# Slots' first weights in two-row and one-row loads over 64 partitions, and four PSUM banks for one attention's values

## The chip, the cores and the metric

One core of a Trainium2 chip runs the whole program in one launch. The metric is the device time of that launch in microseconds. TensorE (PE) has two queues in the profile: PE for matmuls and PEld for weight loads. DVE is VectorE, ACT is ScalarE, POOL is GpSimd, and SP and ACT issue nearly all DMAs. All arithmetic is in float32.

## The reference

The program is a small early-fusion transformer on 16 sequences of 102 tokens (25 image patches and 77 words) with 192 features. Four layers follow the embedding, each an attention-like block and a feed-forward block, with a residual and a layer norm before each. Two blocks matter here.

The first feed-forward block is a soft mixture of 64 slots. Each token is normalised and compared with 64 slot vectors; a softmax over tokens gives the dispatch weights, a softmax over slots the combine weights.

```python
y = einsum('bts,btd->bsd', dispatch_w, x)            # 64 slots of 192 features for each sequence
y = einsum('sif,bsi->bsf', fc1_weight, y) + fc1_bias # own 192 x 768 weights for each slot
y = gelu(y)
y = einsum('sfo,bsf->bso', fc2_weight, y) + fc2_bias # own 768 x 192 weights for each slot
out = einsum('bsd,bst->btd', y, combine_w)
```

Each slot's weights are used for 16 rows only, so the block reads 2 x 64 x 192 x 768 numbers, 75.5 MB, once.

The third attention (layer 2) has 12 heads of 64 features, without biases:

```python
q, k, v = heads(x @ w_q), heads(x @ w_k), heads(x @ w_v)   # 192 -> 12 x 64
out = merge(softmax(q @ k.T / 8) @ v) @ w_o + b_o
```

## The kernel before

Tokens of one sequence lie on 102 partitions. Four sequences make a group, and there are four groups; most stages are loops over groups. Each engine has its own written-out program; semaphores join them. PSUM has eight banks, named by use: `SBANKS` (0, 1) for scores, `TBANKS` (2, 3) for transposes, `OBANKS` (4, 5) for outputs, `XBANKS` (6, 7), and `FBANKS`, which are 2, 3, 6 and 7. `claim(banks)` on TensorE takes the next bank of the tuple and waits until its last contents have been read; `filled` says that it is full; on DVE and ACT `full` waits for that, and `free` gives the bank back.

**Slots.** After the first attention each group's tokens are normalised on DVE (`turn_d`, L1068 multiplies by the norm's weight and writes the features in the order p, k, where feature k x 96 + p becomes column 2p + k). TensorE then makes the dispatch products: for each sequence L2211 with columns 0 to 127 of the tokens as its 128 wide weights and 64 slots as moving columns, and L2215 with columns 128 to 191. ACT copies the result to `YTF` (128 rows, every slot) and `YTH` (even slots on partitions 0 to 63, odd slots on 64 to 127).

The slots are then worked through in 16 quads of four. For each quad, `into_slots` multiplies by first weights (L2232 with the 128 rows, L2236 with the 64 others, L2238 adds the bias), ACT applies Gelu, `turn_hidden` transposes, and one quad later `out_of_slots` (L2248) multiplies by second weights. Three buffers (`QRING`) hold the weights of three quads. The first three quads' weights are loaded beforehand, quads 1 and 2 from the end of the first attention on. From quad 3 on SP loads first weights (`load_first`) as soon as TensorE has given the buffer back (`fc1_used`), and ACT, after Gelu of a quad, loads second weights for the one two ahead (`load_second`).

In DRAM a slot's first weights are rows p of 0 to 96, each with both k, so 2 x 768 numbers: 6 KB that lie together. Row 96 is the bias. `load_first` takes the rows (p, k) as 192 rows of 3 KB. The first 128 of the four slots go to 128 partitions in one DMA of 1536 KB (`FULL`), the last 64 in two DMAs of 384 KB (`HALF`), for the even slots to partitions 0 to 63 and for the odd to 64 to 127. Second weights are one DMA of 2304 KB over 128 partitions, with rows of 4.5 KB for each slot, in two of the three buffers, and four of 576 KB in the third.

**Third attention's values.** In its loop over groups, TensorE makes queries and keys into `FBANKS`, then for each of the four sequences ("batch" `bb`) the values: it claims both `OBANKS`, fills each with 6 heads (384 columns, L1941 for 128 features, L1945 for the other 64), and goes to the next sequence. DVE's `values(V, 64, None)` copies the banks to `V` in the same order (L1006). Then both enter `attention`. Its scores alternate between the banks 0 and 1, and before the first of each TensorE waits until the bank's last contents are read. The product with the values comes five steps later and waits for the last two value banks (`v_moved[-2:]`).

## Time and profile before

| what | value |
|---|---|
| median of 3 runs | 1671.95 us (1662.51 to 1679.76) |
| profiled execution | 1669.09 us |
| its span, first to last instruction | 1667.1 us |
| mean granted TensorE clock | 0.908 of 2.4 GHz |
| busy, share of the span | PE 84%, PEld 59%, DVE 41%, ACT 40%, POOL 23% |
| DMA over the span | 178.84 MB, 107 GB/s |
| slots' stage, first matmul into a slot to the last quad | about 340 to 555 us |
| third attention | about 1070 to 1330 us |

The span is what the profiler sees between the first and the last instruction; 2.0 us of the execution's time lie outside it. A granted clock of 1.00 is 2.4 GHz and 0.50 is 1.2 GHz.

### The profile page before, as it was taken

How to read it: one execution, taken by the hardware profiler on the slowest of the kernel's cores; microseconds unless marked ns; L12 is line 12 of the kernel's file. 1: busy time of each engine (PE TensorE's matmuls, PEld its weight loads, DVE VectorE, ACT ScalarE, POOL GpSimd, SP SyncE). 2: the span in 40 equal slices, each digit the busy share in tenths (PEclk: the TensorE clock that was granted, in tenths of full speed). 3: DMA queues.
4: the chain of work that ended last, by engine and by line, in shares of the span. 5: the costliest groups of instructions: out<-in, count | busy, mean ns of one | idle time of the engine just before them, and what ended most of it. 6: DMA issues, size and time to landing. Idle time of an engine off the chain costs nothing.

```text
span 1667.1 us, 31759 instructions
## 1 busy us (share of the span) xinstructions
PE 1404.5 (84%) x10300; PEld 984.7 (59%) x10300; DVE 683.6 (41%) x2124; ACT 673.0 (40%) x2261; POOL 385.9 (23%) x467
## 2 busy tenths in 40 slices
PE   6799997798566877888899899688988999889994
PEld 4566665633122434555578799454654666679993
DVE  5557756611101277444433622333542423551113
ACT  1667664410000143888842022153654643213331
POOL 5213222200000132232200266220220200124441
PEclk8999996577778778999998899799999999989997
DMA  8434331759999400000004366200000020136653
GB/s 221 138 85 125 91 97 48 232 180 365 301 311 307 140 24 1 1 0 0 0 0 128 105 200 194 75 1 1 0 0 0 16 117 0 31 107 189 187 169 105
DMA packets 96071, 178.84 MB, mean 107 GB/s; under 512 B 36570, under 2 KB 56312, under 8 KB 94336
## 3 DMA queue, kind: packets, MB, share of 16 engines
q1 hardware_dynamic: 81776, 130.75, 27.0%
q10 hardware_dynamic: 7056, 30.67, 5.6%
q0 software_dynamic: 7136, 16.10, 3.1%
q8 instruction: 57, 0.93, 0.3%
q14 instruction: 46, 0.38, 0.1%
HBM read 150.50 MB, written 26.99 MB: 106 GB/s over the span
## 4 chain that ended last, share of the span: by engine, by line
PE 55%; DVE 13%; issue 12%; DMA 9%; ACT 7%; SPq 2%; POOL 1%; DVEq 0%; ACTq 0%; POOLq 0%
DMA WM<-in_fc 8%; PE bank L2444 6%; PE bank L1941 6%; PE bank L2430 4%; PE bank L2014 4%; PE bank L2026 4%; PE bank L2043 3%; PE bank L1945 3%; PE bank L2434 3%; PE bank L2053 3%; PE bank L2104 2%; PE bank L1989 2%; PE bank L2096 2%; ACT ON L1674 2%; ACT KZ L1815 2%
## 5 line engine op out<-in xcount | busy, mean ns | idle before, releaser
L1941 PE MATMUL bank<-XT,AREA 128*128 128x408 f32 (+1 forms) x320 | 138.3, 557 | 23.0 <-ACT XT L1618 10.1
L2014 PE MATMUL bank<-KZ,QT 128*102 128x102 f32 x1152 | 140.2, 261 | 12.2 <-ACT PB L1674 7.4
L700 POOL TENSOR_TENSOR PB<-PB,RCU 102x306 f32<-102x306 f32 x96 | 69.3, 722 | 310.1 <-DVE RCU L964 310.0
L2014 PEld LDWEIGHTS bank<-KZ,QT 128*102 128x102 f32 x1152 | 121.0, 173 | 31.5 <-issue 15.5
L684 POOL TENSOR_TENSOR RS<-VE,expo 102x4 f32<-102x4 f32 (+1 forms) x53 | 53.1, 1002 | 361.7 <-DVE VE L904 303.6
L2444 PE MATMUL bank<-WM,KZ 128*128 x660 | 118.2, 327 | 0.0
L1941 PEld LDWEIGHTS bank<-XT,AREA 128*128 128x128 f32 (+1 forms) x320 | 56.2, 196 | 89.6 <-issue 69.4
L2444 PEld LDWEIGHTS bank<-WM,KZ 128*128 128x128 f32 x660 | 105.7, 190 | 0.4
L1655 ACT ACTIVATE KZ<-bank,AREA 128x128 f32<-128x128 f32 x198 | 54.8, 375 | 121.4 <-PE bank L2434 121.4
L2043 PE MATMUL bank<-PT,V 102*32 102x102 f32 (+1 forms) x1152 | 85.9, 270 | 15.2 <-DVE OT L974 12.3
L2026 PE MATMUL bank<-AREA,OT 128*102 128x192 f32 x384 | 88.9, 345 | 11.3 <-DVE SLOTS L1329 5.3
L1668 ACT ACTIVATE PT<-bank 102x306 f32<-102x306 f32 x192 | 86.3, 452 | 26.2 <-PE bank L2053 25.7
L1784 ACT ACTIVATE QT<-bank 128x512 f32<-128x512 f32 (+1 forms) x32 | 15.7, 491 | 195.9 <-PE bank L2238 195.9
L821 POOL DMA_INDIRECT rows_out<-KZ,TARGET x66 | 66.7, 1010 | 118.3 <-DVE KZ L1474 74.1
L1674 ACT ACTIVATE PB<-bank,MXU 102x102 f32<-102x102 f32 x192 | 65.9, 377 | 64.6 <-DVE MXU L958 64.6
L700 POOL TENSOR_TENSOR ON<-ON,RCU 102x306 f32<-102x306 f32 x96 | 67.1, 699 | 92.5 <-DVE RCU L964 92.2
L2430 PE MATMUL bank<-KZ,SLOTS 128*128 128x128 f32 x660 | 84.6, 275 | 2.6 <-issue 2.6
L2430 PEld LDWEIGHTS bank<-KZ,SLOTS 128*128 128x128 f32 x660 | 82.0, 192 | 3.4 <-issue 3.4
L809 POOL DMA_INDIRECT KZ<-rows_in,TOKEN x66 | 67.7, 1026 | 53.0 <-DVE TOKEN L1451 33.5
L1945 PE MATMUL bank<-XT,AREA 64*128 64x408 f32 (+1 forms) x320 | 78.6, 569 | 0.0
L1267 DVE COPY QT<-bank 128x192 f32<-128x192 f32 x16 | 5.7, 357 | 177.5 <-PE bank L2248 177.5
L958 DVE TENSOR_REDUCE MXU<-bank 102x3 f32<-102x306 f32 x128 | 60.9, 476 | 41.2 <-PE bank L2014 37.4
(347 smaller groups left out, 2807.3 us busy)
## 6 DMA issues: line engine op xcount, KB each, us to landing
AREA<-in_fc SPq DMA_DIRECT2D x10, 1536.0 KB, 20.3
SLOTS<-in_m3w SPq DMA_DIRECT2D x33, 384.0 KB
WM<-in_fc ACTq DMA_DIRECT2D x5, 2304.0 KB, 18.9
WM<-in_fc SPq DMA_DIRECT2D x6, 1536.0 KB, 24.1
AREA<-in_fc ACTq DMA_DIRECT2D x4, 2304.0 KB, 20.5
SLOTS<-in_m1w SPq DMA_DIRECT2D x33, 256.0 KB
AREA<-pos_scratch SPq DMA_DIRECT2D x16, 459.0 KB
pos_scratch<-AREA SPq DMA_DIRECT2D x8, 913.5 KB
```

The source lines that it names most:

```text
L700: pool.tensor_tensor(p, p, scale, ALU.mult).then_inc(sem["probs_ready"], 1)
L809: pool.indirect_dma_start(XG[i % XRING], None, rows_in, bass.IndirectOffsetOnAxis(ap=TOKEN[:, i:i + 1], axis=0), bounds_check=NB * T - 1, ...
L821: pool.indirect_dma_start(rows_out, bass.IndirectOffsetOnAxis(ap=TARGET[:, i:i + 1], axis=0), YO[i % YRING], None, bounds_check=2 * NB * T ...
L1668: free(activation(PT[s % 2][:, 0:HPU, :], src, ACT.Copy), k)
L1674: last = activation(p, p if pos else psum[k][0:T, cols(j)], ACT.Exp, scale=-1.0, bias=MXU[:, s % 4, j:j + 1], accum_out=SMU[:, s % 4, j:j ...
L1941: last = pe.matmul(dst, *whole(n), start=n < 2, stop=False)
L1945: return [pe.matmul(dst, *part(n), start=False, stop=n >= len(outs) - 2) for n, dst in enumerate(outs)]
L2014: last = pe.matmul(psum[k][0:T, cols(j)], QT[:, tile, cols(bb)], KALL[:, unit % per_tile * (HEADS // per_tile) + tile, cols(bb)], start=Tr ...
L2026: last = pe.matmul(psum[PROJBANK][0:T, 0:D], OT[bb % 2][:, m, :], wo[:, m, :], start=m == 0, stop=m == parts - 1)
L2043: last = pe.matmul(psum[k][row:row + rows, cols(tile)], by_head(dv)[:, bb * HEADS + h, :], PT[n % 2][:, j, :], start=True, stop=True)
L2430: pe.matmul(p[:, c], w_all[:, (j * per + m) * 128:(j * per + m + 1) * 128], x[:, 0:TILE], start=m == 0, stop=False)
L2444: last = pe.matmul(p[:, 0:D], HG[i % HRING][:, f * 128:(f + 1) * 128], w2[:, bass.ds(e, 1), f * D:(f + 1) * D].rearrange("p o d -> p (o d) ...
```

## The change

First weights: each slot is loaded by two DMAs. Rows p of 0 to 63, both k together, go as 6 KB rows to 64 partitions (384 KB); rows 64 to 95 go as 64 rows of 3 KB to the other 64 partitions (192 KB). For even slots the two-row part is on partitions 0 to 63, for odd slots on 64 to 127. A quad takes eight DMAs, and `fc1_loaded` counts to 128 for a quad in place of 48. A pair of slots shares one piece of 3 x 768 columns in each buffer: the even slot has columns 0 to 2 x 768, the odd slot from 768 on, or from 2 x 768 on where it has one row. The sizes and the places of the three buffers stay as they are.

`into_slots` has the same matmuls. One takes 128 partitions (one k of the two-row half, and all single rows on the other half), the other takes 64 (the other k of the two-row half). The features of tokens and of slot vectors are put in the matching order: k = 0 of p below 64, then the (p, k) rows of p from 64 on, then k = 1 of p below 64. That takes two DVE operations where one was. In the dispatch products the odd slots need other columns of the tokens than the even, so each sequence has two products with 32 columns where it had one with 64.

Values: the third attention's values use the four banks 4, 5, 0, 1 in turn, on TensorE and on DVE. The product with the values waits for the last four fillings.

```diff
+VBANKS = OBANKS + SBANKS
...
         def load_first(engine, q):
-            j, s = q % QRING, RING * q
-            rows = t["fc1"][s:s + RING].rearrange("s p k f -> (p k) s f")
-            engine.dma_start(FULL[j], rows[0:128]).then_inc(sem[f"fc1_loaded{j}"], 16)
-            for odd in range(2):
-                engine.dma_start(HALF[j][64 * odd:64 * odd + 64], rows[128:D, odd:RING:2]
-                                 ).then_inc(sem[f"fc1_loaded{j}"], 16)
+            j = q % QRING
+            for r in range(RING):
+                slot, odd, there = t["fc1"][RING * q + r], r % 2, FIRST[j][r // 2]
+                engine.dma_start(there[64 * odd:64 * odd + 64, FF * odd:FF * odd + 2 * FF],
+                                 slot[0:64].rearrange("p k f -> p (k f)")).then_inc(sem[f"fc1_loaded{j}"], 16)
+                engine.dma_start(there[64 - 64 * odd:128 - 64 * odd, 2 * FF * odd:2 * FF * odd + FF],
+                                 slot[64:KD].rearrange("p k f -> (p k) f")).then_inc(sem[f"fc1_loaded{j}"], 16)
...
                 for first in range(0, GB * HEADS, per):
-                    k = at.bank(OBANKS)
+                    k = at.bank(OBANKS if dv == 16 else VBANKS)
...
-                weight = nw0[:].rearrange("t (k p) -> t k p", k=2).unsqueeze(1).to_broadcast([T, GB, 2, KD])
-                give(tt(XND[g][:].rearrange("t b (p k) -> t b k p", k=2), X1[:].rearrange("t b (k p) -> t b k p", k=2),
-                        weight, ALU.mult), "xn_ready")
+                weight = nw0[:].rearrange("t (k p) -> t k p", k=2).unsqueeze(1)
+                src = X1[:].rearrange("t b (k p) -> t b k p", k=2)
+                tt(XND[g].rearrange("t b (n c) -> t b n c", c=64)[:, :, 0:3:2, :], src[:, :, :, 0:64],
+                   weight[:, :, :, 0:64].to_broadcast([T, GB, 2, 64]), ALU.mult)
+                give(tt(XND[g][:, :, 64:128].rearrange("t b (p k) -> t b k p", k=2), src[:, :, :, 64:KD],
+                        weight[:, :, :, 64:KD].to_broadcast([T, GB, 2, KD - 64]), ALU.mult), "xn_ready")
...
                 for bb in range(GB):
-                    c = bb * NSLOT
-                    pe.matmul(p[:, c:c + NSLOT], x[:, bb, 0:128], DW[g % 2][:, bb, :], start=True, stop=True)
+                    for odd in range(2):
+                        pe.matmul(p[:, bb * NSLOT + odd:(bb + 1) * NSLOT:2], x[:, bb, 64 * odd:64 * odd + 128],
+                                  DW[g % 2][:, bb, odd:NSLOT:2], start=True, stop=True)
...
-                pe.wait_ge(sem[f"fc1_loaded{j}"], 48 * (q // QRING + 1))
+                pe.wait_ge(sem[f"fc1_loaded{j}"], 128 * (q // QRING + 1))
...
-                    two_banks = [claim(OBANKS) for _ in range(2)]
+                    two_banks = [claim(VBANKS) for _ in range(2)]
...
-                attention(2, 64, wo2, v_moved[-2:])
+                attention(2, 64, wo2, v_moved[-4:])
```

## Rows read from the trace of the kernel before

**Rows 1.** The page's chain that ended last, by line.
```profile
DMA WM<-in_fc 8%; PE bank L2444 6%; PE bank L1941 6%; PE bank L2430 4%; PE bank L2014 4%; PE bank L2026 4%; PE bank L2043 3%; PE bank L1945 3%; PE bank L2434 3%; PE bank L2053 3%; PE bank L2104 2%; PE bank L1989 2%; PE bank L2096 2%; ACT ON L1674 2%; ACT KZ L1815 2%
```

**Rows 2.** The page's DMA issues: count, KB each, us to landing.
```profile
AREA<-in_fc SPq DMA_DIRECT2D x10, 1536.0 KB, 20.3
...
AREA<-in_fc ACTq DMA_DIRECT2D x4, 2304.0 KB, 20.5
...
AREA<-in_fc SPq DMA_DIRECT2D x10, 384.0 KB, 25.0
```

**Rows 3.** Timeline of the issuing queues: start us, us, instruction.
```profile
294.79 0.58 SPq L226 DMA_DIRECT2D AREA<-in_fc  x1
295.40 1.37 SPq L228 DMA_DIRECT2D AREA<-in_fc  x2
...
360.39 0.44 ACTq L239 DMA_DIRECT2D WM<-in_fc  x1
```

**Rows 4.** Windows, slots' stage: busy times, then TensorE clock, DMA share, GB/s.
```profile
297.00:300.50 3.50, 1.26 (x9) 0.90 (x8) 3.08 (x9) 1.36 (x8) 0.20 (x1) 0.50 1.00 394
301.00:304.00 3.00, 2.36 (x15) 2.18 (x13) 1.29 (x10) 1.88 (x10) 2.19 (x3) 0.50 1.06 234
306.50:310.50 4.00, 3.89 (x30) 3.71 (x31) 2.24 (x6) 0.93 (x6) 0.34 (x1) 0.50 1.00 408
381.50:388.50 7.00, 3.66 (x58) 2.45 (x58) 1.82 (x5) 0.38 (x1) 0.00 (x0) 1.00 1.04 297
389.50:396.50 7.00, 6.04 (x22) 1.09 (x26) 0.00 (x0) 0.21 (x1) 0.00 (x0) 0.52 1.02 417
432.00:437.00 5.00, 1.52 (x22) 0.96 (x12) 1.82 (x5) 0.00 (x0) 0.00 (x0) 1.00 1.06 199
350.50:545.50 195.00, 138.09 (x1286) 52.76 (x1285) 24.86 (x68) 13.74 (x28) 0.00 (x0) 0.80 1.01 315
460.00:540.00 80.00, 51.78 (x464) 19.52 (x460) 9.11 (x25) 4.91 (x10) 0.00 (x0) 0.78 1.03 311
```

**Rows 5.** Waits of PE, 350 to 553 us, and its timeline in quads 2 and 3.
```profile
PE bank L2232 <- DMA KZ<-in_fc: 25.4, 4, 8.2
PE bank L2232 <- DMA AREA<-in_fc: 21.1, 3, 7.8
PE bank L2232 <- DMA WM<-in_fc: 11.7, 4, 6.9
...
361.36 1.06 PE L2232 MATMUL bank<-AREA,SLOTS 128*32 128x512 f32 x8
...
369.27 1.07 PE L2232 MATMUL bank<-WM,SLOTS 128*32 128x512 f32 x8
```

**Rows 6.** DMA queues, 365 to 370 us: packets, MB, share of busy time.
```profile
q1 hardware_dynamic: 190, 0.53, 38.8%
```

**Rows 7.** Timeline of one group's dispatch.
```profile
306.61 1.78 PEld L2211 LDWEIGHTS bank<-PT,XN 102*128 102x128 f32 x8 [0.68 <-ACT PT L1773]
306.61 1.97 PE L2211 MATMUL bank<-PT,XN 102*128 102x64 f32 x8 [0.47 <-ACT PT L1773]
...
308.23 0.96 DVE L1068 TENSOR_TENSOR ON<-X,early 102x768 f32<-102x768 f32 x1
```

**Rows 8.** Timeline of third attention's values, first group.
```profile
1091.14 1.25 DVE L1006 COPY V<-bank 102x384 f32<-102x384 f32 x2 [10.81 <-PE bank L1945]
...
1092.45 1.54 PE L1941 MATMUL bank<-AREA,XT 128*102 128x384 f32 x4 [1.34 <-DVE V L1006]
...
1093.91 0.89 PE L1945 MATMUL bank<-AREA,XT 64*102 64x384 f32 x4
...
1102.59 1.15 DVE L1006 COPY V<-bank 102x384 f32<-102x384 f32 x2 [2.51 <-PE bank L1945]
1103.87 1.07 DVE L958 TENSOR_REDUCE MXU<-bank 102x3 f32<-102x306 f32 x2
```

**Rows 9.** Waits over the whole span.
```profile
PE bank L1941 <- DVE V L1006: 16.3, 12, 1.7
```

More of the change, by code:

```diff
@@ L210, in build @@
         HS = HT.rearrange("p k t -> p (k t)")[:, 0:FT * 128].rearrange("p (k t) -> p k t", k=FT)
-        FULL = [buf[:, 0:RING * FF].rearrange("p (s f) -> p s f", s=RING) for buf in (WM, AREA)]
-        HALF = [buf[:, RING * FF:6 * FF].rearrange("p (s f) -> p s f", s=2) for buf in (WM, AREA)]
+        PAIR = 3 * FF
         SECOND = [[buf[:, 6 * FF + r * FT * D:6 * FF + (r + 1) * FT * D] for r in range(RING)] for buf in (WM, AREA)]
@@ L216, in build, with first_rows @@
         flat_of_all = lambda buf, c, n: buf.rearrange("p k t -> p (k t)")[:, c:c + n]
[L217 to L219 removed]
+        FIRST = [[buf[:, 0:PAIR], buf[:, PAIR:2 * PAIR]] for buf in (WM, AREA)]
+        FIRST.append([AREA[:, taken:taken + PAIR], flat_of_all(KT, 0, PAIR)])
+        SECOND.append([WM[:, taken:taken + FT * D], AREA[:, taken + PAIR:taken + PAIR + FT * D],
                        flat_of_all(HT, FF, FT * D), flat_of_all(QT[:], FF + D, FT * D)])
+        def first_rows(j, r, c0, c1):
+            at0 = 2 * FF * (r % 2)
+            rows = slice(64 * (r % 2), 64 * (r % 2) + 64)
+            return FIRST[j][r // 2][:, at0 + c0:at0 + c1], FIRST[j][r // 2][rows, FF + c0:FF + c1]
         def load_first(engine, q):
[L224 to L229 removed]
+            j = q % QRING
[5 more added lines that the diff above has]
+                                 slot[64:KD].rearrange("p k f -> (p k) f")).then_inc(sem[f"fc1_loaded{j}"], 16)
         def load_second(engine, q):
@@ L1035, in unit_slots @@
                 step(dve.reciprocal(RC[0:NSLOT, 0:1], MX[0:NSLOT, 0:1]))
-                give(ts(SL2.rearrange("s (p k) -> s k p", k=2), SL.rearrange("s (k p) -> s k p", k=2),
+                src = SL.rearrange("s (k p) -> s k p", k=2)
+                ts(SL2.rearrange("s (n c) -> s n c", c=64)[:, 0:3:2, :], src[:, :, 0:64],
+                   RC[0:NSLOT, 0:1], slS[:, 0:1], ALU.mult, ALU.mult)
+                give(ts(SL2[:, 64:128].rearrange("s (p k) -> s k p", k=2), src[:, :, 64:KD],
                         RC[0:NSLOT, 0:1], slS[:, 0:1], ALU.mult, ALU.mult), "xn_ready")
@@ L2214, in _ @@
                     for odd in range(2):
-                        last = pe.matmul(p[64 * odd:64 * odd + 64, c:c + NSLOT // 2], x[:, bb, 128:D],
+                        last = pe.matmul(p[64 * odd:64 * odd + 64, c:c + NSLOT // 2], x[:, bb, 128 - 128 * odd:D - 128 * odd],
                                          DW[g % 2][:, bb, odd:NSLOT:2], start=True, stop=True)
@@ L2232, in into_slots @@
                         pe.matmul(o[32 * r:32 * r + 32], YTF[:, NB * s:NB * s + 32],
-                                  FULL[j][:, r, c0:c1], start=True, stop=False)
+                                  first_rows(j, r, c0, c1)[0], start=True, stop=False)
                     for r in range(RING):
@@ L2236, in into_slots @@
                         pe.matmul(o[32 * r:32 * r + 32], YTH[rows, NB * (s // 2):NB * (s // 2) + 32],
-                                  HALF[j][rows, r // 2, c0:c1], start=False, stop=False)
+                                  first_rows(j, r, c0, c1)[1], start=False, stop=False)
                     filled(pe.matmul(o, PICK[:, 128 * q:128 * q + 128], BIAS[:, c0:c1], start=False, stop=True), k)
```

3 lines of the change are left out of this document (removed).

## The prediction

> **What bounds the kernel now.** I read the page's chain first, then windows of the stage that it names, then the timeline of the other places that the diff touches. TensorE is the busiest engine over the span, but the chain by line [rows 1] has as its largest single item the load of the slots' weights, 8% of the span, before any matmul line. The windows [rows 4] show that stage: from 350.5 us, when the first buffer is given back, to 545.5 us the DMA engines are busy without a gap (share 1.01) and move 315 GB/s, 61.4 MB in 195 us, which is the 13 quads after the first three at 2304 KB of first and 2304 KB of second weights each [rows 2]. TensorE needs 7.9 us for a quad at full clock (quads 2 and 3 begin at 361.4 and 369.3 us) and waits 58 us in all for first weights [rows 5]. At the lower clock level (0.50 to 0.52 [rows 4]) it needs at most 16 us, still less than the 17 that I get below for a quad's loads. So a change in the rate of these loads passes straight into the time, and a change in TensorE's work inside the stage doesn't.
>
> The rate isn't one number, and this carries the prediction. SP puts a 128-partition load of 1536 KB and then two 64-partition loads of 384 KB on its queue for each quad [rows 2, 3]. When the queue works alone, 297 to 300.5 us is the wide load: 394 GB/s. Right behind it, 301 to 304 us, are the two narrow ones: 234 GB/s at the same full share [rows 4]; from 352 us on, at the next refill, the pair repeats. The rows in DRAM are 3 KB in both; what differs is the partitions written. Once ACT's queue runs beside it (its loads are all of 128 partitions) the same alternation goes on: 297 GB/s in a stretch of narrow loads, 417 in the next (three of the slow and two of the fast kind by 405 us); later the stretches blur into a steady 311 [rows 4].
>
> **The change, slots' loads.** Eight loads for a quad in place of three, all of them over 64 partitions: four of 384 KB in 6 KB rows, four of 192 KB in 3 KB rows. The 1536 KB at 128 partitions are gone. Two effects are to be priced.
> Longer rows: second weights have 4.5 KB rows, and on SP's queue alone they moved at 408 GB/s [rows 4], against 394 for 3 KB rows. Half as long again bought 3%, within what the edges of such windows are worth, so 6 KB rows get nothing from me; by the same 3% on half the bytes it would be 3 us.
> Narrow loads: while a load writes one half of the partitions, that half takes all of SP's bytes and half of ACT's. In a slow stretch, 365 to 370 us, SP's queue had 39% of the DMA engines' time and so nearly of the bytes [rows 6], ACT's the rest, so the loaded half took 0.39 + 0.305 = 0.69 of 297 GB/s, 205 GB/s. In the new kernel both queues have 2304 KB a quad, so the share is 0.5 + 0.25 = 0.75, and the total 205 / 0.75 = 274 GB/s. SP's queue is alone for the first 10 us (ACT issues first at 360.4 us [rows 3]) and moves 2.3 MB there at 234 GB/s; the other 59.1 MB at 274 take 216 us. Together 226 against 195: **+31 us**, 17 us for a quad. The ends: with 234 GB/s as what a half can take, 312 in total, 199 us, +4; with 199 GB/s, the slowest stretch of narrow loads [rows 4], 265 in total, 233 us, +38. I take the middle value since it is the one measured with both queues running, which is how the stage runs.
> The Trainium skill ("SBUF — State Buffer", Door 1: The DMA port swizzle) says that partitions 0 to 63 reach 8 of the 16 DMA ports and 64 to 127 the other 8, with an asymptote of about 218 GB/s for either half; by that rule, the trace agrees (234). Its page "DMA: Bandwidth & Descriptors" (Rules for kernel authors) speaks against this change: two transfers to disjoint partition halves serialize, one 128-partition transfer is to be used. With its 218 the total would be, as an estimate, 218 / 0.75 = 291 GB/s and the stage +18 us.
> SP's issuing: eight issues at 0.6 to 0.7 us [rows 3] are 5 us a quad, and a quad takes over 14, so the queue stays fed. What is queued behind them on SP is only the next quad's loads. The loads of quads 1 and 2, from 294.8 us on, now need some 22 us for first and 12 us for second weights, until about 330 us; TensorE comes to quad 1 at 350.9. That cover costs nothing.
>
> **The change, dispatch.** Each group's four products with 64 columns become eight with 32, with the same 128 wide weights. Four took 1.97 us, of which weight loading is 1.78 [rows 7]. By columns the eight cost no more; if each needs a weight load as now, they take 3.56, +1.6 us. The chain of this stage runs through this line (its second largest), at half TensorE's clock. I take +1.1, nearer the second, since loading fills nine tenths of the line now: **+4.4 us** for four groups (0 to 6.4). The slot order moved from one DVE operation of 0.96 us to two of together 768 elements a row: some 0.1 us of fixed cost for each of four [rows 7]. With the same split for the slots themselves, at the start under the word gathers, this is **+0.3**. The matmuls into slots keep their number and shapes.
>
> **The change, third attention's values.** The timeline [rows 8] shows the pattern to look for: the products of one batch (2.35 us) fill both banks, DVE copies the two out, and only then does the next batch begin, 1.31 us after the first copy's start; this comes three times a group, with no other engine at work, and I take 3.7 us a group. With four banks batch 1 finds two free ones, batch 2 finds batch 0's emptied during batch 1, and so on: DVE needs 1.25 us in a period of 2.4. All three waits go. Late next is the first score tile: it now shares banks with the last batch, so it starts when the first copy is done (0.6 us) and needs some 0.7 us, where before its reduction started 1.28 us after the first copy's start anyhow, because DVE was copying. That gives back 0.1 us a group. 4 x (3.7 - 0.1) = **-14.4 us**; the wait row [rows 9] has 16.3 us, the far end, and if the scores' wait costs 0.7 us more each, -11.
>
> **Sum.** +31 + 4.7 - 14.4 = +21 us on the profiled execution's 1669.1 (2.0 us of it lie outside the span and don't change), 1690. The median of the runs lies 2.9 us above it (1671.95), so the forecast is **1693 us**, 1.3% slower. Its own range: +4 + 0 - 16.3 = -12 to +38 + 6.5 - 11 = +34, that is 1660 to 1706. One per cent, 17 us, is about what a measurement of this kernel can tell from no change: its three runs differ by that much.
>
> **Rivals.**
> A, the halves overlap. Within a quad the loads go to half A, B, B, A, A, B, B, A of the partitions; spread evenly over 16 engines that is 24 or 12 KB a load, so stretches of 36 KB on one half. If engines are apart by about one stretch, half of them write A while the others write B, and all loads run as the wide ones do, at 417 GB/s: 61.4 MB in 147 us, -48, and with the rest -58: 1614 us. For it: the clean alternation of rates is gone after 460 us [rows 4], as if the engines had come apart. Against: in that state the rate is 311, not 417, though only a sixth of the bytes are in narrow loads. Half way, at 340 GB/s, it gives 181 us, -14, and 1647 us.
> B, the rate stays as it is. The slow stretches are dear now because narrow loads and everything beside them slow down together; if in the blurred state (311 GB/s [rows 4]) the mix no longer matters, the stage takes 59.1 MB / 311 + 10 = 200 us, and at exactly the old rate 195. Then the attention's gain stands against dispatch: -10 us, 1662. For it: 311 is what the second half of the stage does. Against: that state still had two thirds of SP's bytes at 128 partitions.
> C, the slowest engine decides more often. A load counts when its last engine is done, and there are 128 such parts a quad for 48. Should each quad lose 2 us more than its bytes say, 13 quads add 26 us: 1719.
> D, the diff does less than it says: the values' banks bring nothing because something else in the loop takes the slack. The chain is on TensorE and DVE alone there, so I give this little; it would make 1707.
>
> **Chances.** Forecast 0.58, A 0.15 (half of it the half-way case), B 0.17, C and D 0.10. Within the forecast case, about two thirds lie above +1%, nearly all the rest inside 1%. B lies within 1% mostly, with a tail below. So slower by over 1%: 0.39 + 0.10 + 0.01 = 0.50; within 1%: 0.18 + 0.13 = 0.31; faster: 0.19. The range takes in B and leaves out A's full form and the upper part of C: 1657 to 1712.
>
> **What would show it.** In the windows of the changed kernel: from 350 us to the stage's end the share of DMA at 1.0 and the rate at 265 to 290 GB/s with no stretch above 350; the first 10 us near 230; the stage 25 to 38 us longer; the wait for first weights grown from 58 to over 80 us. In the dispatch, the new matmul line at 3 us a group. In third attention, the waits of TensorE for DVE's copies gone and the four batches' products within 10 us. The prediction is wrong at its root if stretches of narrow loads run at 400 GB/s, and wrong in size if the loaded half takes 234 rather than 205 GB/s once both queues run.

## The result and the profile after

The changed kernel takes 1706.5 us (median of 4 runs, 1701.1 to 1710.9) against 1674.8 us for the kernel before in the same session (1662.5 to 1679.8): ratio 1.0193, 95% interval 1.0148 to 1.0237. It is slower by 32 us where 21 were forecast. The profiled execution took 1705.7 us, span 1704.0, against 1669.1 and 1667.1.

I laid the first and last start of a few lines beside each other, before and after, and took the differences, stretch by stretch:

| stretch | before us | after us | difference | forecast |
|---|---|---|---|---|
| start to the first attention's first score sum | 62.9 | 66.8 | +3.9 | 0 |
| from there to its last | 212.6 | 220.4 | +7.8 | 0 |
| from there to the first dispatch transposition | 30.0 | 28.8 | -1.2 | +0.3 |
| dispatch, to the first bias matmul of the slots | 38.2 | 44.6 | +6.4 | +4.4 |
| slots, first to last bias matmul | 208.4 | 244.7 | +36.3 | +31 |
| from there to the third attention's first value copy | 539.0 | 538.8 | -0.2 | 0 |
| third attention, first to last value copy | 204.6 | 187.9 | -16.7 | -14.4 |
| rest | 371.4 | 372.0 | +0.6 | 0 |

The rows sum to the 36.9 us between the spans. Windows of before and of after, in this order (busy times of the engines, then granted clock, DMA share, GB/s):
```profile
18.00:30.00 12.00, 7.27 (x65) 6.31 (x57) 7.60 (x27) 2.58 (x5) 3.15 (x4) 0.77 1.05 246
60.00:205.00 145.00, 130.18 (x1029) 90.09 (x1027) 101.78 (x271) 102.13 (x391) 35.99 (x46) 0.98 0.41 108
380.00:510.00 130.00, 87.05 (x763) 32.34 (x766) 14.58 (x40) 8.59 (x18) 0.00 (x0) 0.78 1.03 319
```
```profile
18.00:30.00 12.00, 5.96 (x74) 4.86 (x65) 6.42 (x28) 2.02 (x4) 1.30 (x3) 0.82 1.05 209
60.00:205.00 145.00, 130.75 (x954) 89.29 (x952) 91.66 (x244) 94.02 (x359) 31.38 (x41) 0.89 0.37 101
364.50:374.50 10.00, 10.00 (x112) 3.93 (x109) 2.94 (x7) 0.98 (x2) 0.00 (x0) 1.00 0.90 204
375.00:400.00 25.00, 15.39 (x176) 6.62 (x174) 3.65 (x10) 1.96 (x4) 0.00 (x0) 0.82 1.02 255
450.00:475.00 25.00, 13.50 (x92) 4.69 (x92) 1.82 (x5) 0.98 (x2) 0.00 (x0) 0.66 1.03 259
525.00:550.00 25.00, 16.89 (x145) 7.25 (x136) 3.65 (x10) 0.98 (x2) 0.00 (x0) 0.70 1.03 270
364.50:590.00 225.50, 147.88 (x1217) 54.30 (x1214) 24.83 (x67) 12.74 (x26) 0.00 (x0) 0.71 1.02 260
380.00:510.00 130.00, 77.06 (x639) 28.39 (x640) 12.55 (x35) 6.86 (x14) 0.00 (x0) 0.70 1.03 262
```
The second line of the table isn't the change's. From 60 to 205 us the granted clock is 0.89 where before had 0.98, with the same instructions to run. Over the fourteen profiles of this study this attention takes 212.5 to 213.5 us in seven and 218.0 to 222.6 us in the other seven. From 75 to 260 us the granted clock was 0.96 to 0.98 in the first seven and 0.92 to 0.94 in the others. Kernels with and without the change stand in both groups, and the longest is dispatch_split, which is before to the letter up to there. So some 8 us of the 37 belong to this execution.

The first line is the change's, and I had not seen it. SP issues the weights of the first quad at the very start, at 17.9 us, right behind the first attention's own and ahead of the transfers of its position table. From 18 to 30 us the rate is 209 GB/s for 246, and the first store of the table starts at 50.8 us for 48.8. Sorted by this one property, the profiles part without an overlap: the eight kernels with narrow loads throughout begin the score sums at 65.0 to 67.2 us (median 66.5), the six others at 61.8 to 64.2 (63.2). That is +3.3 us. How the delay gets from the loads to the score sums isn't shown: in loads_alone that first store starts at 49.0 us, and the sums still begin 2.1 us later than in before.

What the profiles put on the change is thus +3.3 + 6.4 + 36.3 - 16.7 = +29 us. The medians say +32, with 7 us to either side. A stretch in a single profile has a spread of its own: before, values_alone and dispatch_split have the same loads in the stage of the slots and take 208.4, 210.4 and 206.6 us there, after and loads_alone 244.7 and 241.2. I read nothing from differences under 4 us.

In the stage of the slots the picture is the one forecast, in kind. The first 10 us read 204 GB/s at a share of 0.90, 227 at a full one; from there on the share is 1.02 or more, the rate is 255 to 273 GB/s in every stretch of 25 us up to 600 us and 260 over the whole; the fast stretches of the kernel before, 417 GB/s [rows 4], are gone. The page names the same bound, one point larger. Its chain by line, and its DMA issues (count, KB each, us to landing):
```profile
DMA WM<-in_fc 9%; PE bank L2458 6%; PE bank L1954 5%; PE bank L2444 4%; PE bank L2027 4%; PE bank L2039 3%; PE bank L2056 3%; PE bank L2448 3%; PE bank L2066 3%; PE bank L1958 3%; PE bank L2109 2%; PE bank L2117 2%; ACT ON L1687 2%; ACT KZ L1828 2%; PE bank L1901 1%
...
AREA<-in_fc SPq DMA_DIRECT2D x30, 384.0 KB, 28.1
...
AREA<-in_fc ACTq DMA_DIRECT2D x4, 2304.0 KB, 28.9
AREA<-in_fc SPq DMA_DIRECT2D x30, 192.0 KB, 29.6
```
TensorE's waits for first weights, 364 to 606 us (us in total, times, longest), sum to 78.3 us against 58 [rows 5]:
```profile
PE bank L2246 <- DMA AREA<-in_fc: 32.1, 4, 9.7
PE bank L2246 <- DMA KZ<-in_fc: 23.8, 4, 11.2
PE bank L2246 <- DMA WM<-in_fc: 22.4, 4, 9.8
```
A load of 384 KB takes 28.1 us to land, longer than the 20.3 that one of 1536 KB took [rows 2]: it stands in a queue that is never empty. So the number to read is the rate of the stage, not the landing time of a load.

The dispatch of one group (compare [rows 7]):
```profile
317.19 3.49 PEld L2224 LDWEIGHTS bank<-PT,XN 102*128 102x128 f32 x16 [0.68 <-ACT PT L1786]
317.19 3.62 PE L2224 MATMUL bank<-PT,XN 102*128 102x32 f32 x16 [0.47 <-ACT PT L1786]
...
320.74 0.94 PEld L2229 LDWEIGHTS bank<-PT,XN 102*64 102x64 f32 x16
```
Sixteen records for eight, 0.22 us each as before: the line is all weight loading, and half the columns make none of it shorter.

The values of the third attention, first group, in time order, and the first reduction behind them (compare [rows 8]):
```profile
1144.09 1.25 DVE L1013 COPY V<-bank 102x384 f32<-102x384 f32 x2 [10.32 <-PE bank L1958]
...
1146.28 1.54 PE L1954 MATMUL bank<-AREA,XT 128*102 128x384 f32 x4
1146.38 1.24 DVE L1013 COPY V<-bank 102x384 f32<-102x384 f32 x2 [1.04 <-PE bank L1958]
...
1148.74 1.15 DVE L1013 COPY V<-bank 102x384 f32<-102x384 f32 x2 [1.13 <-PE bank L1958]
...
1151.03 1.15 DVE L1013 COPY V<-bank 102x384 f32<-102x384 f32 x2 [1.13 <-PE bank L1958]
1152.46 1.07 DVE L965 TENSOR_REDUCE MXU<-bank 102x3 f32<-102x306 f32 x2 [0.28 <-PE bank L2027]
```
Now DVE waits for TensorE (1.0 to 1.1 us before each copy) and not the other way; a batch takes 2.3 us, and the first reduction starts 8.37 us after the first copy where it took 12.73 [rows 8]. The row of waits for DVE's copies before values [rows 9] is gone. A smaller one is new, before the first score of each of the four groups, which now needs a bank that held values:
```profile
PE bank L2027 <- DVE V L1013: 2.9, 4, 0.7
```
With it the first reduction starts 1.43 us after the group's last pair of copies begins, where it was 1.28.

### The profile page after: what moved, and what is told of

Same layout as the page of the kernel before. It is cut to its first block, busy times and chain, and to the rows that moved or that the text cites. A ratio compares the mean times of both kernels' runs of the same rounds, so it can differ in the third digit from the quotient of the medians.

```text
span 1704.0 us, 31920 instructions
## 1 busy us (share of the span) xinstructions
PE 1434.6 (84%) x10332; PEld 1000.4 (59%) x10332; DVE 684.5 (40%) x2129; ACT 671.8 (39%) x2261; POOL 385.2 (23%) x467
## 3 DMA queue, kind: packets, MB, share of 16 engines
q10 hardware_dynamic: 7056, 30.67, 6.9%
## 4 chain that ended last, share of the span: by engine, by line
PE 50%; issue 16%; DVE 12%; DMA 11%; ACT 6%; SPq 3%; POOL 1%; DVEq 0%; ACTq 0%; POOLq 0%
DMA WM<-in_fc 9%; PE bank L2458 6%; PE bank L1954 5%; PE bank L2444 4%; PE bank L2027 4%; PE bank L2039 3%; PE bank L2056 3%; PE bank L2448 3%; PE bank L2066 3%; PE bank L1958 3%; PE bank L2109 2%; PE bank L2117 2%; ACT ON L1687 2%; ACT KZ L1828 2%; PE bank L1901 1%
## 5 line engine op out<-in xcount | busy, mean ns | idle before, releaser
L2056 PE MATMUL bank<-PT,V 102*32 102x102 f32 (+1 forms) x1152 | 85.8, 270 | 16.6 <-DVE OT L981 13.7
## 6 DMA issues: line engine op xcount, KB each, us to landing
AREA<-in_fc SPq DMA_DIRECT2D x30, 384.0 KB, 28.1
```

The lines of the kernel that those rows point to most:

```text
L2056: last = pe.matmul(psum[k][row:row + rows, cols(tile)], by_head(dv)[:, bb * HEADS + h, :], PT[n % 2][:, j, :], start=True, stop=True)
```

## The experiments

Twelve kernels ran besides these two. "Stage" is the time from the slots' first to last bias matmul, "rate" that of the window from 380 to 510 us. Ratios are to the kernel before, timed in the same session. Where an edit changes the number of loads, the count that TensorE waits for (`fc1_loaded`) changes with it; the code cuts below leave that out.

| kernel | stage us | rate GB/s | time us | ratio (interval) |
|---|---|---|---|---|
| before | 208.4 | 319 | 1675 | 1 |
| after | 244.7 | 262 | 1706.5 | 1.0193 (1.0148 to 1.0237) |
| values_alone | 210.4 | 313 | 1652.3 | 0.9888 (0.9837 to 0.9940) |
| loads_alone | 241.2 | 270 | 1724.3 | 1.0333 (1.0274 to 1.0392) |
| narrow_3kb | 234.3 | 285 | 1697.4 | 1.0162 (1.0106 to 1.0217) |
| half_wide | 162.3 | 418 | 1627.0 | 0.9726 (0.9674 to 0.9779) |
| two_queues | 260.6 | 249 | 1710.6 | 1.0214 (1.0173 to 1.0254) |
| by_halves | 254.2 | 260 | 1715.1 | 1.0258 (1.0221 to 1.0296) |
| dispatch_split | 206.6 | 325 | 1680.2 | 1.0048 (1.0024 to 1.0072) |
| after_one_queue | - | - | 1702.4 | 1.0139 (1.0070 to 1.0208) |
| before_one_queue | 210.6 | 313 | 1687.3 | 1.0091 (1.0062 to 1.0120) |
| narrow_8 | 233.9 | 282 | 1703.6 | 1.0185 (1.0139 to 1.0231) |
| rows_cut | 236.5 | 281 | 1691.0 | 1.0128 (1.0066 to 1.0189) |
| wide_values | 162.3 | 418 | 1606.8 | 0.9610 (0.9566 to 0.9655) |

For half_wide the rate is that of 380 to 500 us and for wide_values that of 360 to 480, since their loads end earlier.

### The three edits apart

**values_alone**: before with only this part of the diff.
```
-                    two_banks = [claim(OBANKS) for _ in range(2)]
+                    two_banks = [claim(VBANKS) for _ in range(2)]
```


> Only the value banks of the third attention change; the slots' loads are the old ones. My theory (each of three batches a group no longer waits for DVE's two copies, little is given back at the first score): 14 to 17 us faster, 0.9 to 1.0%. Rival (the first score tiles now wait for the copies and give most of it back): under 6 us.


It took 1652.3 us, 1.1% less than before. First to last value copy is 187.9 us, as in after, 16.7 us less than before. The 22 us between the medians are more than that and than the 14 to 17 that I expected; their interval (10 to 27 us) holds both.

**loads_alone**: after with OBANKS back in the places of VBANKS.


> The new slots' loads, feature order and dispatch products, with the old value banks. Theory (loads over 64 partitions are limited by the half they write): the changed kernel plus 14 to 17 us, so 2.8 to 3.2% above the kernel before; windows of the stage at 260 to 270 GB/s from its second refill to its end. Rival (what else was added, chiefly dispatch and the first 300 us, carries the loss): the stage into the slots is less than 20 us longer.


1724.3 us, 3.3% more than before, with the stage at 241.2 us and the dispatch as in after. The stage accounts for 33 us, the dispatch for 6, the start for 2 to 3; the profiled execution is 46 us over before's, of which another 3.9 us lie behind the last value copy (375.3 us for 371.4). The ratio of 1.0333 is 56 us (46 to 66), above the 2.8 to 3.2% that I expected though within its interval; the profile is of the fastest of four executions, and what is over 46 us I can't put in a place. The rival (a stage less than 20 us longer) fails.

**dispatch_split**: before with the dispatch's first matmul alone split.
```
-                    pe.matmul(p[:, c:c + NSLOT], x[:, bb, 0:128], DW[g % 2][:, bb, :], start=True, stop=True)
+                    for odd in range(2):
+                        pe.matmul(p[:, bb * NSLOT + odd:(bb + 1) * NSLOT:2], x[:, bb, 0:128],
+                                  DW[g % 2][:, bb, odd:NSLOT:2], start=True, stop=True)
```


> The kernel before with one edit: the dispatch's full-row matmul of 64 columns is issued as two of 32, even and odd slots, as after does; rows, loads and VectorE's copies as before. Theory of the prediction: the eight groups take 4.4 us longer (30.1 to 34 to 35 us from the first to the last transposition of the dispatch weights), the time 0.2 to 0.4% up, within what can be measured. Rival (the 5 us that after's groups took longer came from VectorE's split product or from the clock): 30 to 31 us.


There are four groups, not eight as I wrote; between the first and last transposition lie three of them. That distance went from 30.1 to 35.1 us, the same as in after (35.1), and to the slots' first bias matmul from 38.2 to 44.6, also as in after. So TensorE's split is the whole of it, 1.65 us a group and 6.6 in all, at the upper end of the 34 to 35 us expected. The time grew by 0.48% (0.24 to 0.72%), 8 us, which agrees. The split of DVE's product (0.96 us before, two operations of together 1.03 us after) doesn't show in the stage. Its timeline:
```profile
315.88 3.49 PEld L2211 LDWEIGHTS bank<-PT,XN 102*128 102x128 f32 x16 [0.68 <-ACT PT L1773]
315.88 3.63 PE L2211 MATMUL bank<-PT,XN 102*128 102x32 f32 x16 [0.47 <-ACT PT L1773]
317.51 0.96 DVE L1068 TENSOR_TENSOR ON<-X,early 102x768 f32<-102x768 f32 x1
```

### Partitions or rows: narrow_3kb, half_wide, narrow_8, rows_cut

**narrow_3kb**: before, its 1536 KB load cut into two over 64 partitions each; rows of 3 KB, layout and matmuls stay.
```
-            engine.dma_start(FULL[j], rows[0:128]).then_inc(sem[f"fc1_loaded{j}"], 16)
+            for h in (slice(0, 64), slice(64, 128)):
+                engine.dma_start(FULL[j][h], rows[h]).then_inc(sem[f"fc1_loaded{j}"], 16)
```


> The kernel before with one edit: the 1536 KB load over 128 partitions is cut into two of 768 KB over 64 partitions each. Rows stay at 3 KB, order, dispatch and matmuls stay. Theory (the partitions written set the rate, not the length of the rows nor the number of loads as such): all first loads run as the narrow ones do, about 265 GB/s with ACT's queue beside, the stage 30 to 40 us longer, 2 to 2.4% slower. Rival 1 (6 KB rows or the eight loads are what costs): no change within 5 us. Rival 2 (long stretches on one half let the two halves come apart): faster than the changed kernel's stage.


The stage grew by 26 us to 234.3, the time by 1.6%, less than the 30 to 40 us and 2 to 2.4% that I expected, at 285 GB/s for some 265. No row got longer and no byte was added, and narrow_8 below shows that the number of loads doesn't matter: the partitions that a load writes do this. My rival 2 asked for a stage shorter than after's, and it is, but not for the reason given there (long stretches on one half): narrow_8 has short ones and the same stage. One window of it:
```profile
380.00:510.00 130.00, 89.96 (x672) 32.42 (x664) 14.59 (x40) 6.86 (x14) 0.00 (x0) 0.67 1.04 285
```

**half_wide**: the other way. The slots' last rows are laid out in DRAM so that both 384 KB loads of before become one of 768 KB over 128 partitions, rows of 3 KB.
```
-            for odd in range(2):
-                engine.dma_start(HALF[j][64 * odd:64 * odd + 64], rows[128:D, odd:RING:2]
-                                 ).then_inc(sem[f"fc1_loaded{j}"], 16)
+            engine.dma_start(HALF[j], t["fc1_last"][q].rearrange("s p f -> p s f")).then_inc(sem[f"fc1_loaded{j}"], 16)
```


> The kernel before with one edit: the last 64 rows of the four slots lie in DRAM in the order of the 128 partitions and are one load of 768 KB over 128 partitions in 3 KB rows, in place of two over 64. Theory (partitions set the rate): no slow stretches are left, 400 to 420 GB/s from the first refill on, the stage 45 us shorter if only the loads bound it, 2.5 to 2.9% faster. Rival (the slow stretches come from something else in those rows, such as their place in DRAM): the same rates as before.


The stage fell by 46 us to 162.3, the time by 2.7%. The rate doesn't vary any more:
```profile
380.00:400.00 20.00, 15.03 (x180) 6.87 (x176) 3.88 (x12) 1.96 (x4) 0.00 (x0) 1.00 1.03 419
400.00:450.00 50.00, 42.69 (x363) 16.09 (x364) 5.55 (x16) 3.92 (x8) 0.00 (x0) 0.73 1.03 418
450.00:500.00 50.00, 40.91 (x422) 16.25 (x424) 9.04 (x25) 4.78 (x10) 0.00 (x0) 0.93 1.03 419
```
The DMA share is 1.03 here and 1.02 in after: the same full share stands for 418 and for 260 GB/s. Busy says nothing of how much is moved.

**narrow_8**: narrow_3kb with its four loads cut in two by slots, in after's order and sizes.
```
+            for r in range(RING):
+                odd = r % 2
+                h, o = slice(64 * odd, 64 * odd + 64), slice(64 - 64 * odd, 128 - 64 * odd)
+                s0 = 2 * (r // 2)
+                engine.dma_start(FULL[j][h, s0:s0 + 2], rows[h, s0:s0 + 2]).then_inc(sem[f"fc1_loaded{j}"], 16)
+                engine.dma_start(HALF[j][o, r // 2:r // 2 + 1], rows[128:D, s0 + 1 - odd:s0 + 2 - odd]
+                                 ).then_inc(sem[f"fc1_loaded{j}"], 16)
```


> narrow_3kb with each of its four loads of a quad cut in two by slots: eight loads of 384 and 192 KB in after's order of sizes and halves, but with rows of 3 KB throughout and before's layout and matmuls. It keeps rows apart from number of loads: after's stage is 245 us at 262 GB/s, narrow_3kb's 234 at 285. If the number of loads or their order makes that difference, this one takes 242 to 250 us; if the 6 KB rows make it (or lines of matmuls that differ), 232 to 237.


Stage 233.9 us at 282 GB/s, as with four loads: neither the number of loads nor after's order of sizes and halves counts. (Another order does, see by_halves.)
```profile
380.00:510.00 130.00, 85.33 (x648) 30.35 (x652) 12.76 (x35) 6.86 (x14) 0.00 (x0) 0.68 1.04 282
```

**rows_cut**: after, each load of 6 KB rows cut in two by columns; the places in memory and the matmuls stay.
```
-                engine.dma_start(there[64 * odd:64 * odd + 64, FF * odd:FF * odd + 2 * FF],
-                                 slot[0:64].rearrange("p k f -> p (k f)")).then_inc(sem[f"fc1_loaded{j}"], 16)
+                for k in range(2):
+                    engine.dma_start(there[64 * odd:64 * odd + 64, FF * (odd + k):FF * (odd + k + 1)],
+                                     slot[0:64, k]).then_inc(sem[f"fc1_loaded{j}"], 16)
```


> The kernel after, with each load of 64 rows of 6 KB cut in two by columns, 64 rows of 3 KB each: twelve loads a quad in place of eight, the same memory places and matmuls. narrow_8 has after's order and sizes at 3 KB rows and before's layout, and takes 234 us at 282 GB/s against after's 245 at 262. If the length of the rows makes that difference, this one takes 232 to 238 us in the stage at 278 to 286 GB/s, and 1693 to 1700 us in all; if it is the places in memory or the matmuls, it stays at 243 to 248; if SP, now with twelve issues a quad, becomes the limit, over 250.


Stage 236.5 us at 281 GB/s: 8 us less than after's, 5 less than loads_alone's, whose loads are after's. Two windows, one with SP's queue alone (3 KB rows), one with both:
```profile
299.50:304.50 5.00, 1.96 (x11) 1.60 (x12) 4.40 (x16) 1.55 (x9) 1.01 (x1) 0.50 0.97 236
...
380.00:510.00 130.00, 79.84 (x672) 29.34 (x676) 12.76 (x35) 7.85 (x16) 0.00 (x0) 0.74 1.04 281
```
and of loads_alone, SP's queue alone with 6 KB rows among them:
```profile
297.00:302.00 5.00, 1.76 (x10) 1.40 (x10) 4.40 (x17) 1.44 (x8) 1.01 (x1) 0.50 1.01 235
302.00:307.00 5.00, 4.36 (x26) 3.75 (x24) 3.15 (x21) 2.31 (x10) 2.45 (x3) 0.50 1.03 221
```
On a queue alone these short windows are too uneven to tell. Windows of 10 us over first weights alone read 220, 227 and 230 GB/s with 3 KB rows (narrow_3kb, narrow_8, rows_cut) and 231 and 229 with 6 KB rows in two thirds of the bytes (after, loads_alone): no loss. Beside the other queue the rates are 281 to 285 with 3 KB rows and 262 and 270 with the longer ones, 4 to 8% less, and the stages 233.9 to 236.5 against 241.2 and 244.7 us. So the pair of neighbouring rows in one row of the load, the first thing that the change does, is a loss of its own of 5 to 10 us in the stage. The time alone doesn't show it: 1.0128 (1.0066 to 1.0189) and after's 1.0193 (1.0148 to 1.0237) overlap. Why is open; where it falls is seen from the queues at the end of the next part.

### What makes a narrow load slow: two_queues, by_halves, after_one_queue, before_one_queue

**two_queues**: after, but from the fourth quad on SP issues the loads to partitions 0 to 63 and ACT those to 64 to 127.
```
-                load_first(sp, q)
+                load_first(sp, q, (0,))
...
+                if q + QRING < QUADS:
+                    act.wait_ge(sem[f"fc1_used{q % QRING}"], q // QRING + 1)
+                    load_first(act, q + QRING, (1,))
```


> The kernel after, but from the fourth quad on SP issues only the loads to partitions 0 to 63 and ACT those to partitions 64 to 127, so that both halves are written at the same time. Theory (a load that writes 64 partitions is slow because it uses half of the ways into the memory, and two such loads side by side use all of them): the rate in the refill stretch goes from 268 towards the 418 GB/s of half_wide, the stage of the slots (first to last bias matmul) from 245 to 170 to 200 us, the time from 1706 to 1640 to 1665. Rival (each packet of such a load is slow whatever runs beside it, or the 16 engines are what is shared): the stage stays at 235 to 250 and the time at 1700 to 1712. Rival 2 (ACT's four more issues a quad block its Gelu, each held back 3 to 4 us as SP's are): the rate rises but the stage stays above 215.


This one went against my theory: in place of 1640 to 1665 us it took 1710.6 us, by its interval the same as after and within what the rival gave. The profiled execution, with a stage of 260.6 us, is the longest of four (1725.3 us; the others took 1701.0 to 1713.6), so that the stage is typically longer than after's isn't shown. Its windows tell two things apart:
```profile
367.00:382.00 15.00, 15.00 (x184) 6.73 (x182) 3.65 (x10) 1.96 (x4) 0.00 (x0) 1.00 1.03 273
384.00:398.00 14.00, 8.94 (x102) 3.81 (x94) 1.82 (x5) 0.38 (x1) 0.00 (x0) 0.98 1.03 273
402.00:405.00 3.00, 2.34 (x32) 1.49 (x36) 0.00 (x0) 0.00 (x0) 0.00 (x0) 0.50 1.06 218
380.00:510.00 130.00, 66.97 (x631) 29.36 (x632) 12.19 (x34) 6.21 (x14) 0.00 (x0) 0.74 1.03 249
```
From 367 to 382 us nearly all traffic is narrow loads, SP's to one half and ACT's to the other, 129 and 143 GB/s. All partitions are being written, and the rate is 273 GB/s, not 418. From 384 to 398 SP loads a half and ACT second weights over 128 partitions: 273 again. From 402 to 405 ACT is alone with a narrow load: 218. So two halves side by side give 1.2 times what one gives, not twice. The balance did the rest no good: ACT's queue now carries 3456 of the 4608 KB a quad, SP's is done early (its loads of 384 KB to AREA land in 10.0 us, ACT's in 27.6), and narrow loads then run alone.

**by_halves**: after, each quad's four loads to the lower half first, then the four to the upper, by a loop over the halves around the loads.


> The kernel after, all on SP, but each quad's eight loads in another order: first the four to partitions 0 to 63, then the four to partitions 64 to 127 (after took them in turns of slots, 0, 64, 64, 0). Sizes, rows and queue are as in after. If the order within a quad is what makes the new layout 7 us slower in the stage than narrow_3kb, the stage falls from 245 to 236 to 240; if neighbouring loads to the two halves overlapped a little in after and don't here, it grows to 250 or more; if only the number of partitions of each load counts, it stays within 3 us of 245 and the time within 0.5% of 1706.


Stage 254.2 us, 10 us longer than after's and 13 longer than loads_alone's. Of the three answers that I had offered it is the second: in after neighbouring loads to the two halves would overlap a little. The order is shown to cost this, the overlap as its cause is argued. The rate from 380 to 510 us is nearly after's (260 for 262). The page's slices of 43 us show the loss, after first, by_halves second: in the four slices from 427 us on (values 11 to 14) 2, 3, 5 and 2% less.
```profile
GB/s 212 126 97 99 104 77 71 226 100 262 265 261 264 268 175 1 1 1 0 0 1 0 140 144 196 142 64 1 0 0 0 0 130 0 20 90 204 177 175 103
```
```profile
GB/s 202 134 95 103 105 75 67 226 109 262 260 253 252 263 127 57 0 1 0 0 1 0 139 119 201 156 66 1 0 0 0 0 129 0 20 83 204 179 176 102
```

**after_one_queue, before_one_queue**: from the fourth quad on SP issues the second weights, behind the same quad's first weights, and ACT's `load_second` is gone (not in the cut).
```
                 load_first(sp, q)
+                sp.wait_ge(sem[f"fc2_used{q % QRING}"], q // QRING)
+                load_second(sp, q)
```


> The kernel after, with the slots' second weights of the fourth quad on issued by SP behind the same quad's first weights, and not by ACT: one queue carries both. Loads that write 64 partitions and loads that write 128 then take turns instead of running side by side. Theory (the slow loads go at 234 GB/s and the others at 418, and the two queues side by side cost extra, because each holds up the other's packets): 2.36 MB of each a quad take 10.1 and 5.6 us, 300 GB/s in place of 262, the stage from 245 to 213 to 222 us, the time from 1706 to 1675 to 1685. Rival (side by side costs nothing of its own, and after's narrow loads are simply slower than 234): 262 GB/s and 240 to 248 us. Against both: fewer loads in flight and a later issue of the second weights could lengthen it beyond 250.

> The kernel before with the same edit. Narrow loads are a sixth of its bytes (0.79 of 4.72 MB a quad). In turns they would take 3.4 and 9.4 us, 370 GB/s in place of 319: the stage from 208 to 180 to 187 us and the time to 1645 to 1655 if running side by side has a cost of its own; 205 to 212 us and no change of the time if it has none.


Neither gains what was asked. The first takes 1702.4 us (1688.3 to 1730.4), by its interval the same as after; its profiled execution is the longest, 26 us above the next, so I don't read the stage from it. The second takes 0.9% more than before; its stage is 210.6 us at 313 GB/s, in the fastest of its seven executions. Its windows show that one queue doesn't keep the two kinds apart for good:
```profile
396.00:400.00 4.00, 4.00 (x17) 0.67 (x18) 0.00 (x0) 0.00 (x0) 0.00 (x0) 0.50 1.02 412
404.00:407.00 3.00, 3.00 (x30) 1.51 (x33) 0.00 (x0) 0.38 (x1) 0.00 (x0) 0.50 1.03 198
412.00:415.00 3.00, 2.27 (x12) 0.40 (x16) 0.00 (x0) 0.00 (x0) 0.00 (x0) 0.50 1.01 409
417.00:423.00 6.00, 6.00 (x40) 1.78 (x42) 0.00 (x0) 0.98 (x2) 0.00 (x0) 0.50 1.04 214
380.00:510.00 130.00, 94.36 (x753) 34.25 (x754) 14.58 (x40) 7.85 (x16) 0.00 (x0) 0.71 1.03 313
```
Fast and slow stretches follow each other as in before, and the slow ones last longer than the narrow bytes alone: from 417 to 423 us 1.28 MB moved, where a quad has 0.79 MB in narrow loads. Served one after the other, 0.79 MB at 234 and 3.93 MB at 418 GB/s would take 12.8 us a quad, 370 GB/s; measured are 313, 15.1 us. The narrow sixth of the bytes costs 15.1 - 9.4 = 5.7 us, as if it moved at 138 GB/s. In narrow_3kb the same sum gives 4.72 MB / 285 = 16.6 us, less 5.6 for the wide half, 11.0 us for 2.36 MB, 215 GB/s; in after 18.0 - 5.6 = 12.4 us, 190 GB/s. So the first narrow loads are the dearest per byte, which is why half_wide, which takes out the last of them, gains 46 us, and the change, which adds twice as many bytes as that took away, loses only 36.

That narrow loads slow the wide ones beside them can be read directly. Queue q10 is ACT's. It carries the same bytes in all kernels but the three in which this part moved loads between queues: second weights of quads 3 to 15, all over 128 partitions. The pages' rows for it (packets, MB, and the time that the packets took as a share of 16 engines' span), for half_wide, before, narrow_3kb, rows_cut and after:
```profile
q10 hardware_dynamic: 7056, 30.67, 4.6%
q10 hardware_dynamic: 7056, 30.67, 5.6%
q10 hardware_dynamic: 7056, 30.67, 6.2%
q10 hardware_dynamic: 7056, 30.67, 6.3%
q10 hardware_dynamic: 7056, 30.67, 6.9%
```
Share times 16 engines times span, over 7056 packets, is 170, 212, 238, 241 and 267 ns for the same packets (narrow_8 238, loads_alone 256). So a wide load's own packets take up to 1.6 times as long beside narrow loads, and 6 to 12% longer when two thirds of SP's bytes come in 6 KB rows. SP's own packets don't pay for the longer rows: from 380 to 510 us they had 48.0% of the engines' time for 15.70 MB in after and 53.6% for 17.48 MB in rows_cut, 64 us of engine time for each MB in both.

### The version that follows

**wide_values**: half_wide with the value banks, and none of the slots' new layout.


> half_wide and the four value banks together, with none of the slots' new layout. The two edits are 500 us apart and should add: 1627 less 17 to 22 us is 1605 to 1610, ratio to before 0.957 to 0.963; the stage of the slots 162 us, the third attention's copies 188 us. If the second gain were given back by what comes later (the routed part's loads), it would stay near 1627.


1606.8 us, ratio 0.961 (0.957 to 0.966), 65 us below before in the same session (1672.2 us) and some 100 below after. The two gains add, as expected. Its window and chain by line:
```profile
360.00:480.00 120.00, 92.62 (x1013) 39.03 (x1012) 20.05 (x55) 10.78 (x22) 0.00 (x0) 0.93 1.03 418
```
```profile
PE bank L2443 7%; PE bank L1940 5%; DMA AREA<-in_fc_last 5%; PE bank L2429 5%; PE bank L2013 4%; PE bank L2042 3%; PE bank L2025 3%; PE bank L2433 3%; PE bank L2052 3%; PE bank L1944 3%; PE bank L2103 2%; ACT ON L1673 2%; ACT KZ L1814 2%; PE bank L1887 2%; PE bank L2095 2%
```
The load is still in the chain, at 5%, but no longer at its head. That share alone is no measure of the stage: narrow_8's page has 5% for the same item, at a stage of 234 us.

## Why the prediction was right, and where its steps were off

**The bound.** Right. In narrow_3kb and half_wide only these loads were changed, and +26 and -46 us in the stage came out as 1.62% and -2.74%, +27 and -46 us of the whole. The granted clock in the stage fell from 0.78 to 0.70, beside a TensorE that waits more. That this cost nothing is an estimate: at the lower level a quad takes TensorE at most 16 us, and its loads took 18.0 in after.

**The slots' refills, +31, measured +36.3.** The direction and most of the size come from the step "narrow loads", and narrow_3kb shows it alone: +26. The step that was off is "6 KB rows get nothing from me": rows_cut gives back 8 us when they are cut, so the sum is 26 to 28 for the partitions and 5 to 10 for the rows. I had asked only whether longer rows gain; the row that I priced them by [rows 4] was of 128-partition loads on a queue alone, where narrow loads show no loss by 6 KB rows either, and no row had long rows in narrow loads beside another queue. (The prediction's "half the bytes" for the 6 KB rows is two thirds of SP's bytes and a third of the stage's.) The signs that the prediction named came out so: the rate 260 to 262 GB/s for 265 to 290, the first 10 us 204 (227 at a full share) for 230, the stage +36 for 25 to 38, the waits 78.3 us for over 80, the dispatch line 3.6 us a group for 3.

**The loads left out, +3.3.** The prediction priced the refills and found the loads of quads 1 and 2 covered; the first quad's, at the start, it didn't name. It had looked at "what is queued behind them on SP" only for the stage, and at the start that is the first attention's table.

**The mechanism of the rate.** "The loaded half takes 205 GB/s" gave 274 in total for 260 measured (0.75 of it is 195). The 205 itself mixes two windows: the share of 39% is that of 365 to 370 us, whose own rate is 283 GB/s, and 297 is the rate from 381.5 to 388.5 us. With one window's numbers the same sum gives 0.695 x 283 = 197 for the half and 262 in total, just what after has from 380 to 510 us. That is luck, since the picture doesn't hold: when two_queues spread narrow loads over both halves at once, no half had more than 143 of 273 GB/s, and it was no faster than one half beside the wide loads. Nor does a limit of a half distinguish rows of 3 and of 6 KB, which moved at 285 and 262. The Trainium skill ("DMA: Bandwidth & Descriptors", Rules for kernel authors) says that two transfers to disjoint halves serialize and that one over 128 partitions is to be used. The advice is what half_wide shows (319 to 418 GB/s). "Serialize" is nearly what two_queues shows: 273 with both halves against 218 to 236 with one. The 218 GB/s for a half that the prediction set beside its 234 is a little low for this kernel: 10 us of narrow loads alone moved at 220 to 231. What in the hardware a 64-partition load lacks isn't settled here.

**Rival A** (overlap, 1614 us) fails by the steady 260 and by two_queues; by_halves may hold a trace of it, 10 us of the stage. **Rival B** (the rate stays) fails: 319 became 262. Its reason, that the mix no longer matters in the blurred state, is the one half_wide contradicts most. **Rival C** (the slowest of many parts decides) fails: narrow_8 has twice narrow_3kb's loads in the same time. **Rival D** fails: the 16.3 us of waits before values went.

**Dispatch, +4.4, measured +6.4 to 6.6.** The mechanism was right; the size was at the far end that I had written down (each product needs a weight load: +1.6 a group, measured +1.65). My value lay between the ends for no reason that a row gave, since 1.78 of 1.97 us already was weight loading [rows 7]. **DVE's split, +0.3**: 0.07 us a group in DVE's own time and nothing in the stage (35.1 us with it and without).

**Third attention, -14.4, measured -16.7.** The far end again, by the size of the waits. I took 3.7 us a group, where the row that I quoted gives three times 1.31, 3.9, and the wait row 16.3 / 4 = 4.1 [rows 8, 9]; the copies of the four groups are now 17.2 us closer together, 4.3 a group. What I gave back for the shared score banks did come: 0.15 us a group for the 0.1 forecast, and the new waits of 2.9 us took the place of 2.5 us of waits for ACT.

**The sum.** +21 forecast, +29 by the profiles' stretches, +32 by the medians (25 to 40). The misses are +5 in the stage, +3 at the start, +2 in the dispatch and -2 in the attention.

## What to carry to other kernels

When a stage is bound by loads, compare the rate of its stretches, not the DMA share, which read 1.03 at 418 and at 249 GB/s; a stretch at half rate beside one at full rate names the load to rewrite. Lay weights out in DRAM so that every load writes all 128 partitions, leftovers of a second row tile too: taking the narrow bytes from 2.36 to 0.79 MB a quad was worth 26 us in the stage, taking the last 0.79 away 46. Splitting a matmul by columns costs a full weight load for each part wherever loading fills its line, and a wait of TensorE for copies out of two banks is had back almost whole by two more banks that are idle then.

## What was unexpected of the hardware

- Two queues that load the two halves of the partitions at the same time move 273 GB/s together, against 218 to 236 for one and 418 for loads over all 128.
- Narrow loads slow wide ones beside them: a packet of the same wide loads took 170 ns with no narrow loads, 212 with a sixth of the bytes in them and 238 to 267 with half. A sixth of the bytes in narrow loads took the rate from 418 to 319 GB/s, where one after the other it would be 370.
- With 6 KB rows in two thirds of the bytes of the 64-partition loads, the two queues together moved 4 to 8% less than with 3 KB rows (262 and 270 against 281 to 285 GB/s); on a queue alone nothing was lost (229 to 231 against 220 to 230).
- The first attention, with the same instructions, took 212.5 to 213.5 us in seven profiles and 218.0 to 222.6 us in seven others; from 75 to 260 us the granted clock was 0.96 to 0.98 in the first and 0.92 to 0.94 in the others.
